# Splitting layer 1's sixteen token chunks 8 and 8 in place of 10 and 6

## The reference

```
x  = L0_attn_x                                        # 32 x 256 x 128 = 8192 tokens
xn = layernorm(x)
x  = x + causal_attention(xn) + moe0(xn)              # 16 experts, best 2 of each token, + a shared one
xn = layernorm(x)
x  = x + delta_rule_attention(xn) + moe1(xn)          # moe1: 4 experts in use, best 2 of each token

moe1: w, i = top_k(softmax(xn @ gate_w.T), 2);  w /= sum(w)
      out  = sum over the two of  w * (silu(xn @ w1[e]) * (xn @ w3[e])) @ w2[e]      # hidden size 704
delta_rule_attention: a scan over the tokens of each sequence, 16 heads of 8 x 8 state
```

## Time and profile before

| what | value |
|---|---|
| time, median of 3 runs | 2041.62 us (2035.27 to 2042.34) |
| the profiled execution's own time | 2032.93 us |
| its span, first to last instruction | 2031.2 us |
| mean granted TensorE clock | 0.86 |
| busy: PE / DVE / ACT / POOL | 78% / 68% / 48% / 44% of the span |

### The profile page before, as it was taken

The page is one execution under the profiler, slowest core; times in us unless marked ns, Lnnn a source line. Parts: engine busy times, 40 slices in busy tenths (PEclk is TensorE's granted clock), DMA queues, the critical chain, the costliest instruction groups (busy, mean ns, idle before and its releaser), DMA issues.

```text
span 2031.2 us, 29771 instructions
## 1 busy us (share of the span) xinstructions
PE 1585.3 (78%) x9764; PEld 994.8 (49%) x9766; DVE 1389.9 (68%) x2616; ACT 978.8 (48%) x1600; POOL 899.0 (44%) x973
## 2 busy tenths in 40 slices
PE   2953977888788999878774868999999977789950
PEld 2740444455455555444332545666665655456530
DVE  5765645566556666676687837888888778688822
ACT  3720544555444555545554444566566544456410
POOL 4237436623645223657888247112121147711126
PEclk9875888999877899787867779999999988989985
DMA  6944678778756766656445555566566557755423
GB/s 212 281 127 158 174 203 240 216 206 212 201 160 191 193 163 167 158 135 172 128 119 155 180 162 171 158 197 173 182 188 184 156 170 222 224 168 171 140 84 87
DMA packets 277946, 354.43 MB, mean 174 GB/s; under 512 B 32273, under 2 KB 204305, under 8 KB 272417
## 3 DMA queue, kind: packets, MB, share of 16 engines
q1 hardware_dynamic: 237600, 287.92, 50.0%
q0 software_dynamic: 17056, 33.66, 6.0%
q10 hardware_dynamic: 23136, 30.94, 4.5%
HBM read 197.48 MB, written 122.68 MB: 158 GB/s over the span
## 4 chain that ended last, share of the span: by engine, by line
PE 44%; DVE 13%; issue 11%; ACT 8%; POOL 8%; another core or an unknown queue 6%; SPq 5%; DMA 4%; ACTq 0%; DVEq 0%; POOLq 0%
PE Y L1060 7%; PE R L819 6%; PE R L821 5%; PE R L820 5%; POOL gat L1345 3%; PE R L835 3%; PE Y L955 3%; PE R L920 2%; POOL xs_dram L1366 2%; DVE state L2020 2%; ACT probs L1532 2%; PE R L901 2%; PE R L895 2%; PE R L940 2%
## 5 line engine op out<-in xcount | busy, mean ns | idle before, releaser
L1919 DVE TENSOR_REDUCE row_max<-R 128x6 f32<-128x768 f32 x256 | 241.6, 953 | 153.8 <-PE R L920 96.2
L1377 POOL TENSOR_SCALAR_AFFINE_SELECT probs<-probs 128x512 f32<-128x512 f32 x256 | 169.4, 662 | 342.2 <-ACT probs L1532 337.7
L1366 POOL DMA_INDIRECT xs_dram<-sc_in,pos x256 | 262.1, 1024 | 127.7 <-issue 62.9
L1386 POOL TENSOR_TENSOR o_acc<-o_acc,read 128x512 f32<-128x512 f32 x112 | 144.7, 1292 | 391.4 <-DVE read L2030 390.4
L1345 POOL DMA_INDIRECT gat<-ys_dram,pos x256 | 253.6, 990 | 140.8 <-issue 69.2
L1060 PE MATMUL Y<-hid,fd 128*128 128x512 f32 x456 | 244.7, 618 | 38.7 <-DVE hid L2068 27.2
L1532 ACT ACTIVATE probs<-R 128x768 f32<-128x768 f32 x256 | 205.4, 808 | 135.5 <-PE R L943 86.6
L819 PE MATMUL R<-fhl,fw 128*128 128x512 f32 x418 | 230.3, 551 | 26.7 <-issue 17.7
L2068 DVE TENSOR_TENSOR hid<-R,sil 128x512 f32<-128x512 f32 x228 | 156.0, 687 | 62.2 <-ACT sil L1651 32.7
L1651 ACT ACTIVATE sil<-R 128x512 f32<-128x512 f32 x190 | 113.2, 596 | 142.0 <-PE R L821 117.3
L2020 DVE TENSOR_TENSOR_SCAN state<-dw 128x512 f32<-128x512 f32 x128 | 174.2, 1361 | 1.9 <-ACT dw L1620 0.6
(11 more groups left out here) (268 smaller groups left out, 3538.2 us busy)
## 6 DMA issues: line engine op xcount, KB each, us to landing
fw<-wf SPq DMA_DIRECT2D x38, 1408.0 KB
q_rows<-kq SPq DMA_DIRECT2D x128, 256.0 KB
fx<-xs_dram SPq DMA_DIRECT2D x86, 256.0 KB
xs_dram<-gat SPq DMA_DIRECT2D x24, 512.0 KB, 4.5
qk_dram<-qk_parts SPq DMA_DIRECT2D x32, 384.0 KB
Q<-qk_dram SPq DMA_DIRECT2D x64, 192.0 KB
K<-qk_dram SPq DMA_DIRECT2D x64, 192.0 KB
fw<-wf SPq DMA_DIRECT2D x96, 128.0 KB
```

The lines of the kernel that those rows point to most:

```text
L1366: pool.indirect_dma_start(xs_dram[g], bass.IndirectOffsetOnAxis(ap=pos[l][g][a][:, col:col + 1], axis=0), sc_in[:, n % 2, t * P:(t + 1) * ...
L1377: pool.affine_select(out=diag, in_=diag, compare_op=ALU.is_ge, fill=0.0, base=0, pattern=[[0, 2], [0, 2], [1, P]], channel_multiplier=-1)\
L1919: dve.tensor_reduce(row_max[:, b, h2, :, :], pair[:, :].rearrange("p (g c t) -> p g c t", g=2, t=P)[:, :, 0:3, :], AX.X, ALU.max).then_inc ...
```

## The change

Layer 1's groups become 8 and 8 chunks, as layer 0's are.

```
-CHUNKS = ((8, 8), (10, 6))
+CHUNKS = ((8, 8), (8, 8))
```

## The result

8 and 8 is slower: 2067.5 us against 2038.4, medians of four runs each, ratio 1.0195 (1.0139 to 1.0251); in five more runs of both on one chip the ratio was 1.0115 (1.0074 to 1.0156), some 23 us. The forecast was +7.5.

The account below looks back on a forecast made before the run. No single engine was taken to bound the whole: PE bounds the steady state, POOL's indirect transfers four other stages. 20.8 - 12.7 - 1.2 + 0.6 = +7.5 us gave 2049 us on the median, range 2027 to 2067.

Parts of the forecast that it names:

- The tail: After the last expert tile's store: 64 gathers in place of 48, 16 x 1.30 us, +20.8 us that nothing hides.
- The wait at the start: Before the first expert tile's load: the wait for the first group's scatter goes away, -12.7 us if attention ends unchanged.
- the 955 forecast: First group's 64 scatters during attention, with 32 gathers in the same stretch: finished about 955 us, well ahead of 1092.
- Does attention end when it did? ... I take 0: End of layer 1's attention: its last store doesn't move, 0 taken, with 16.4 us to both sides.
- rival 2: Start not earlier: attention loses up to 16.4 us from 767 on, deciding at 12.7; +20 us, 2062 us; chance 0.16.
- Its bound by the last chunk: Attention's end: last chunk took 61.7 us, chunk 10 took 45.3, so at most 16.4 us gained or lost.
- rival 3: Faster: attention's last chunk regains 16.4 us and loses nothing earlier; -8.9 us, 2033 us; chance 0.15.
- The second scatter: Early expert stage: 64 scatters in place of 48 cost +5.8 to +6.7 us; PE near 64 of 89 us busy.
- 16 fewer: -5.8 to -9.1 us: First group's gathers in the expert stage: 64 in place of 80, priced at 0.365 to 0.57 us each.
- Both alarms: Signs of error: last attention store, or first tile's load to last tile's store (850.2 us), moves by over 6 us.
- Rival 1: Second scatter stays on the path one for one, 20.8 in place of 6.2: +22 us, 2064 us; chance 0.20.
- rival 4: POOL's transfers stretch beside DVE: the 16 more scatters exceed all seen, 2070 us or above; chance 0.03.

Follow-up runs that it names:

- late_scatter: 8 and 8 kernel with the first group's route and scatter given the due times of the kernel before; ratio to the kernel before 1.0034.
- a_spread_sc0: 8 and 8 kernel with the first group's 64 scatters handed out evenly; ratio to the kernel before 0.9934.
- x_none: 8 and 8 kernel with the first group's 64 gathers each replaced by a short fill without a transfer; ratio to the kernel before 0.9962.
- b_none: Kernel before (10 and 6) with its first group's 80 gathers each replaced by a short fill without a transfer; ratio to the kernel before 0.9857.
- b_spread_both: Kernel before (10 and 6) with the first group's 80 scatters and 80 gathers both handed out evenly; ratio to the kernel before 0.9997.
- a_spread_g: 8 and 8 kernel with the first group's 64 gathers handed out evenly; ratio to the kernel before 0.9967.
- x_busy: 8 and 8 kernel with the first group's 64 gathers each replaced by a small POOL power operation without a transfer; ratio to the kernel before 0.9991.
- x_rows: 8 and 8 kernel with each of the first group's 64 gathers fetching 16 rows in place of 128; ratio to the kernel before 1.0105.
- after_again: The 8 and 8 kernel unchanged, profiled a second time and timed in five more runs; ratio to the kernel before 1.0115.

## Why the prediction was wrong

- **The tail** was right: +20.6 us for +20.8, at the pitch of the earlier trace rows.
- **The wait at the start** went away: -12.8 for -12.7, the first tile's load within 5 us of the last attention store, as written. The tenth is luck, as the two pairs give -12.3 and -13.3. The last scatter was done at 924 and 934 us, ahead of the 955 forecast.
- **"Does attention end when it did? ... I take 0"** failed. It ended 7.0 us later (5.8 over all profiles, above), and the 0 was taken without a row of its own. That is rival 2's place and direction, within its 16.4 us, but short of the 12.7 at which it decides, so the start came 5.8 us earlier after all. Its bound by the last chunk missed the size of what moved: chunk 11 lost 49 us and the later chunks regained most of it. That the crowded scatters did it, late_scatter and a_spread_sc0 show; spread, they let attention end 28 us before that of the kernel before (699.9 us after the third store, 728.0 there), beyond rival 3's 16.4.
- **The second scatter**: +4.4 for +5.8 to +6.7, right within what profiles can tell. PE worked 79% of its stretch, not 64 of 89 us (72%).
- **"16 fewer: -5.8 to -9.1 us"** failed, and by more than any other step: +4.0. I divided a stretch's whole loss by its number of gathers and multiplied by another number. Neither step holds: about half of that loss stands without any gather (x_none, b_none), and the rest, 25 us for 64 and 26 for 80, goes with the dense run, since spread gathers take no more time than none.
- Both alarms that I named went off in the mean of the two profiles: the last attention store moved by 7.0 us, from the first tile's load to the last tile's store it was 8.5 us more. I named the new order as the cause. Of the 8.5 us, 4.4 are the second scatter, nearly as forecast; the rest and attention's 7.0 us are hardly more than two profiles of a kernel differ. That the order costs, by how densely it sets indirect transfers, the spread runs show, and not these two differences.
- **Rival 1** (the second scatter one for one) and **rival 4** fell. A scatter of the changed kernel takes 1.03 us on average and 1.96 at most, with DVE busy 67% of the span (68% before); the 3.1 us that the Trainium skill ("SBUF — State Buffer", section "SBUF: two separate sides") gives for a transfer beside a copy are seen nowhere here. The harm of transfers from POOL is real, but most of it falls on other engines and not on POOL's own time.

## What to carry to other kernels

Don't price a stage per transfer by dividing its loss by their count: take the transfers out once and see what remains, since half of the loss here wasn't theirs, and 64 and 80 lost about the same. When a planner fills every free place of an engine with indirect transfers, ask it for an even pitch that still ends before the next consumer: against the same split without it that was worth 1.2 to 3.5% here, where moving the split cost 1.2%. b_spread_both, whose scatters ended too late, gained nothing. And measure stages from a point ahead of the change, since the opening alone moved 10 us between two profiles of one kernel.

## What was not expected of the hardware

Indirect transfers issued from POOL in rows, at a pitch of 1.25 us and some 22 in 30 us, make PE, ACT and DVE stand together for 5 to 13 us at a time, and the profile names nothing that ends these waits: 84.6 us of them in 150 us, added up over the three engines. Neither the rows moved (an eighth of them: 84.5 us) nor POOL's time (a power operation in their places: 2.7 us) is what does it. Handed out, one in 3.7 us on average ((1791.6 - 1557.8) / 63 in a_spread_g) and six in a row at most, it is 13.0 us.

The kernel says which semaphore each of these instructions waits for, and the trace holds many of the semaphores' updates. By these, the first stall above is POOL's time after all: DVE waits for the square root that stands behind ten gathers and ends at 1591.3, and ACT and PE wait behind DVE. x_busy has such a hold too, and its DVE waits 3.4 us there. The second is of another kind. PE and DVE wait for ACT, and ACT waits for PE: the matmuls whose result it copies (L835) are recorded as done at 1596.75, but their semaphore rises at 1606.00. Four later matmuls, recorded as done from 1597.45 to 1599.30, raise theirs within 0.15 us, from 1610.94 on. This is what sets dense gathers apart. From 1550 to 1700, 12 of the 111 updates that the trace holds of PE's semaphores come over 1 us behind the recorded end of their matmul, by up to 13.5 us; in x_rows 16 of 112, in x_none 0 of 159, in x_busy 0 of 160, in a_spread_g 1 of 156, by 1.5 us. In the kernel before (1637 to 1787) it is 15 of 94. No update of ACT, DVE or POOL is late in any of these.

Why PE's signals come late is open. The ends of matmuls are modelled in the profile, so whether the work or only its signal is late can't be told for sure. Two suspects fall at this stall. ACT also waits for the landing of the store two tiles before, and that had landed by 1548.26. The Trainium skill ("Runtime: NRT & Kernel Launch", section "Instruction fetch mechanics") says that every engine's instructions are fetched ahead by DMA in pieces of 16 KiB; but the two instruction queues moved nothing from 1596.4 to 1637.6, so no fetch that came late let ACT go at 1606. In attention the same waits came and went with the crowding (96.7 and 33.3 us from 767 to 924; late updates of PE 34 of 135 in after_again, 12 of 164 in a_spread_sc0, up to 8.9 and 2.9 us), but there the transfers were only spread and not replaced.
